# Moving the down-weight splits, re-ordering the drain and ending on a pair tile in an attention + mixture-of-experts kernel

## The reference

```python
x = x + xattn(ctx, layernorm(x), side)         # x: 4 x 1024 x 256, ctx: 4 x 77 x 256, 16 heads
xf = layernorm(x).reshape(4096, 256)
probs = softmax(xf @ Wr)                        # 9 experts
topk_w, topk_idx = top_k(probs, 2)              # then normalised to sum 1
gate = silu(xf @ Wg[e]); hidden = gate * (xf @ Wu[e])     # 256 -> 704
out = sum over the 2 experts e of topk_w * (hidden @ Wd[e])
x = x + out
```

## Time and profile before

| | |
|---|---|
| median of 3 runs | 832.52 us (832.21 to 832.76) |
| profiled execution | 832.81 us, its span 831.2 us |
| granted clock of PE | 0.996 of full over the span |
| PE busy | 795.7 us, 96% |
| DVE, ACT, POOL busy | 667.6, 625.8 and 380.2 us |

### The profile page before, as it was taken

The page is one execution under the profiler, slowest core; times in us unless marked ns, Lnnn a source line. Parts: engine busy times, 40 slices in busy tenths (PEclk is TensorE's granted clock), DMA queues, the critical chain, the costliest instruction groups (busy, mean ns, idle before and its releaser), DMA issues.

```text
span 831.2 us, 19592 instructions
## 1 busy us (share of the span) xinstructions
PE 795.7 (96%) x6037; PEld 754.9 (91%) x6037; DVE 667.6 (80%) x1620; ACT 625.8 (75%) x1966; POOL 380.2 (46%) x534
## 2 busy tenths in 40 slices
PE   7999999999999999879999999999999999999993
PEld 6866999999999999779999999999999999999993
DVE  6778888888888887887878788787888877888771
ACT  4578898889889888655777778777778777777771
POOL 3021377688778767763334233442343424424232
PEclk9999999999999999999999999999999999999998
DMA  8065900401310020656575182255752654556211
GB/s 288 20 152 147 268 32 30 150 27 40 122 52 33 33 85 27 210 155 171 148 199 120 25 262 46 47 170 152 225 153 46 194 159 119 133 142 160 40 23 23
DMA packets 78044, 96.14 MB, mean 116 GB/s; under 512 B 10680, under 2 KB 65140, under 8 KB 77940
## 3 DMA queue, kind: packets, MB, share of 16 engines
q1 hardware_dynamic: 64179, 75.94, 29.7%
q0 software_dynamic: 13760, 18.96, 12.4%
HBM read 108.14 MB, written 31.29 MB: 168 GB/s over the span
## 4 chain that ended last, share of the span: by engine, by line
PE 82%; DVE 4%; issue 3%; SPq 3%; POOL 2%; DMA 2%; ACT 2%; DVEq 1%; POOLq 0%
PE banks L344 23%; PE banks L345 22%; PE banks L346 22%; PE banks L1357 4%; PE banks L1337 2%; PE banks L1514 2%; PE banks L1371 2%; PE banks L1311 1%; DMA expert_in<-blank 1%; POOL expert_in L878 1%; PE banks L1287 1%; ACT prob L1046 1%; DVEq L1544 1%; PE banks L1323 1%; SPq L657 1%
## 5 line engine op out<-in xcount | busy, mean ns | idle before, releaser
L344 PE MATMUL banks<-tok_t_hi,wgt_hi 128*128 128x256 f32 x704 | 199.7, 284 | 4.8 <-DVE hid_f L1988 1.9
L346 PE MATMUL banks<-tok_t_hi,wgt_lo 128*128 128x256 f32 x704 | 198.0, 281 | 0.0
L345 PE MATMUL banks<-tok_t_lo,wgt_hi 128*128 128x256 f32 x704 | 197.9, 281 | 0.0
L941 POOL DMA_INDIRECT result<-res,tok_id x72 | 117.7, 1635 | 161.2 <-ACT res L1179 129.9
L1046 ACT ACTIVATE prob<-banks,row_min 128x77 f32<-128x77 f32 x512 | 161.8, 375 | 2.9 <-DVE row_min L1711 2.9
L1980 DVE TENSOR_TENSOR wgt_lo<-wgt,wgt_hi 128x704 fp32r<-128x704 f32 x174 | 150.4, 905 | 14.7 <-ACT wgt_hi L1122 14.7
L344 PEld LDWEIGHTS banks<-tok_t_hi,wgt_hi 128*128 128x128 f32 x704 | 134.3, 191 | 7.9 <-issue 5.9
L346 PEld LDWEIGHTS banks<-tok_t_hi,wgt_lo 128*128 128x128 f32 x704 | 133.5, 190 | 0.0
L345 PEld LDWEIGHTS banks<-tok_t_lo,wgt_hi 128*128 128x128 f32 x704 | 133.4, 189 | 0.0
L1122 ACT ACTIVATE wgt_hi<-wgt 128x704 fp32r (+1 forms) x174 | 130.6, 801 | 0.5
L1046 ACT ACTIVATION_READ_ACCUMULATOR prob<-banks,row_min 128x1 f32 x512 | 131.0, 257 | 0.0
(11 more groups left out here) (274 smaller groups left out, 2131.3 us busy)
## 6 DMA issues: line engine op xcount, KB each, us to landing
wgt<-in_L_ffn_Wg SPq DMA_DIRECT2D x29, 704.0 KB
wgt<-in_L_ffn_Wu SPq DMA_DIRECT2D x29, 640.0 KB
wgt<-in_L_ffn_Wd SPq DMA_DIRECT2D x29, 640.0 KB
tok<-expert_in SPq DMA_DIRECT2D x32, 258.0 KB, 3.4
spare_wgt<-in_L_ffn_Wg SPq DMA_DIRECT2D x9, 704.0 KB, 4.2
spare_wgt<-in_L_ffn_Wu SPq DMA_DIRECT2D x9, 640.0 KB, 5.9
spare_wgt<-in_L_ffn_Wd SPq DMA_DIRECT2D x9, 640.0 KB, 4.3
valmat_f<-valmat_dram SPq DMA_DIRECT2D x4, 1197.0 KB, 6.3
```

What stands on the lines that cost most here:

```text
L344: nc.tensor.matmul(to, a[0], b[0], start=first, stop=False)
L345: nc.tensor.matmul(to, a[0], b[1], start=False, stop=False)
L346: return nc.tensor.matmul(to, a[1], b[0], start=False, stop=last)
L941: nc.gpsimd.indirect_dma_start(out, bass.IndirectOffsetOnAxis(ap=tok_id[:, t % NOTES, a:a + 1], axis=0), res[i][:, a, :], None, compute_op ...
```

## The change

1. **Down splits.** Pieces 4 and 5 of tile t are split in tile t's own step, behind `tok_move`/`tok_rest` in unit 1 of a pair, or behind the hidden split of a single; before, this stood in unit 2 of step t - 1, ahead of the last hidden split of t - 1. They have their own semaphores (`down_hi`, `down_split_made`).
2. **Drain.** DVE's end of phase 1 is written out by hand (`drain`): the early gate-and-up splits and `tok_rest(0)` are elsewhere, `allot` of the last block stands behind `hidden(0, 1)`, `table_ends` is apart from `table_counts`, and the other table parts stand later between tile 0's and tile 1's work. PE takes `ranks(T - 3)` behind `gate_up(0, 0)` and `down(0)` behind `gate_up(1, 2)`. The exponential of the gates of the last two blocks goes from ACT to POOL, as a power of e, and ACT loads the silu table once, behind the probabilities' rounding.
3. **Tails.** SP stores all nine; eight of them are now 128 rows.
4. **SP's order.** The first single's weights are loaded in the step of tile 4, not ahead of tile 3's refills; gate-and-up refills go before down refills.
5. **End.** The last tile is a pair. Its two result blocks lie in two banks, its `down` starts ahead of the last hidden unit, and each block is scaled and added as soon as it is done.

The core of the diff goes through SP, POOL, ACT, PE (`down` of the last tile) and DVE:

```diff
-SINGLES_AFTER = (2, 6, 10, 13, 17, 21, 24, 28)
+SINGLES_AFTER = (2, 5, 9, 12, 16, 19, 23, 26)
...
-            for e in range(POOL_TAILS, E):
-                store_tail(sp, e, tails_stored)
+            for e in range(E):
+
+                blocks = WB if e == E - 1 else 1
+                row = sp.value_load(tail_row[0:1, e:e + 1], min_val=0, max_val=E * REGION - W)
+                sp.dma_start(expert_in[bass.ds(row, blocks * P), :].rearrange("(a p) d -> p a d", p=P), blank[:, 0:blocks, :]
+                             ).then_inc(tails_stored, 16)
...
+                refill_gate_up(t)
+                if t == EARLY + 1:
...
+                    load_single_gate_up(0)
+                    load_single_down(0)
                 if t > EARLY:
                     refill_down(t - 1)
-                refill_gate_up(t)
...
+            def gap_power(t, c):
...
+                nc.gpsimd.tensor_tensor(scaled[:], scaled[:], y_rstd[:], ALU.mult).then_inc(gap_scaled, 1)
...
+                nc.gpsimd.tensor_tensor(power[:], euler[:], scaled[:], ALU.pow).then_inc(gap_exp_done, 1)
...
+            def round_down(t, src):
+
+                act.wait_ge(*weights_loaded(t, False))
+                if t > EARLY:
+                    act.wait_ge(down_done, t - 1)
+                for p0, p1 in PIECES[2 * KT:]:
+                    nc.scalar.activation(wgt_hi[half_of(t)][:, p0:p1], src[:, p0:p1], ACT.Copy).then_inc(down_hi, 1)
...
                 for u in range(UNITS):
                     silu(t, u)
-                    if ahead:
+                    if ahead and u < UNITS - 1:
                         round_pieces(t + 1, u, src)
                     hid_round(t, u)
-                    if u == UNITS - 2 and t:
-                        tok_move(t + 1)
+                    if u == UNITS - 2:
+                        if t < NT - 1:
+                            tok_move(t + 1)
+                        if t >= EARLY:
+                            round_down(t, own)
...
+                if t == NT - 1:
+                    inner(0, 0, FC - 2)
+                    pe.wait_ge(res_ready, BLOCKS_TO[t])
+                    inner(1, 0, FC - 2)
+                    pe.wait_ge(hid_ready, UNITS_TO[t + 1])
+                    for a in range(blocks):
+                        inner(a, FC - 2, FC - 1)
+                        last_inner(a).then_inc(down_done, 1)
+                    return
...
+            for s in range(T + 1):
+                step(s, s)
+            drain()
+            table_ends()
+            hid_rest(0, 0)
             table_counts()
...
             hidden(0, 2)
             hid_rest(0, 1)
-            table_rows()
+            table_tiles()
             hidden(1, 0)
-            hid_rest(0, 2)
             early_down_rest()
+            hid_rest(0, 2)
+            tok_rest(2)
+            settle()
+            hidden(1, 1)
+            table_experts()
+            table_rows()
```

More of the change, by code:

```diff
@@ L15 @@
+import math
 from contextlib import ExitStack
@@ L557, in late_vals, with result_bank @@
             return range(SOON_VALS + s * LATE_VALS, min(SOON_VALS + (s + 1) * LATE_VALS, VALS))
[L559 to L564, removed]
+        def result_bank(t, a):
+            if t == NT - 1 and a:
+                return bank[7 - t % 2][:, 0:D]
+            return bank[6 + t % 2][:, a * D:(a + 1) * D]
         block = ctx.enter_context(nc.Block())
@@ L1084, in step @@
                     softmax_exp(s, c, 2)
-                if has(s, 3):
+                if s == T:
+                    tok_move(0)
+                    early_round(0)
+                if has(s, 3) and s - 3 < T - POOL_GAPS:
                     act.wait_ge(gap_ready, s - 2)
@@ L1208, in single_step @@
                 if not last:
-                    round_pieces(t + 1, 2, src)
-            for s in range(T + 4):
+                    round_down(t, spare_wgt[:])
+            for s in range(T + 2):
                 step(s, s)
+            silu(0, 0)
+            early_down_round()
+            hid_round(0, 0)
             silu(0, 1)
-            hid_round(0, 0)
+            tok_move(1)
             hid_round(0, 1)
@@ L1217, in _ @@
             hid_round(0, 2)
-            for t in range(1, NT):
+            silu(1, 0)
+            hid_round(1, 0)
+            silu(1, 1)
+            tok_move(2)
+            silu(1, 2)
+            hid_round(1, 1)
+            hid_round(1, 2)
+            res_move(0)
+            for t in range(2, NT):
                 if t == EARLY:
@@ L1458, in step @@
                     val(m)
-                if has(s, 3) and s < T + 2:
+                if has(s, 3) and s != T and s < T + 2:
                     ranks(s - 3)
@@ L1531, in single_step @@
                 hid_turn(t)
-            for t in range(1, NT):
+            for u in range(UNITS - 1):
+                gate_up(1, u)
+            tok_turn(2)
+            gate_up(1, UNITS - 1)
+            down(0)
+            for t in range(2, NT):
                 if is_pair(t):
@@ L1776, in step @@
                     find_most()
-                if s == T + 1:
-                    early_rest(1)
-                elif s == T + 2:
-                    hidden(0, 0)
                 if has(s, 2):
@@ L1804, in step @@
                     prob_rest(s - 2, c - 2, NG - 1)
+                if s == T:
+                    tok_rest(0)
+                    early_rest(0)
                 if has(s, -1):
@@ L2071, in _ @@
             table_slots()
-            hidden(1, 1)
+            hidden(1, 2)
             hid_rest(1, 1)
-            tok_rest(2)
             single_segments()
-            hidden(1, 2)
             hid_rest(1, 2)
```

212 lines of the change are left out of this document (134 added, 78 removed).

## The result

| | before | after |
|---|---|---|
| median | 832.52 us (832.21 to 832.76, 4 runs by now) | 822.07 us (820.95 to 823.93, 4 runs) |
| profiled execution, its span | 832.81, 831.2 us | 822.03, 820.3 us |
| ratio of times | | 0.9876, 95% interval 0.9864 to 0.9888 |

The account below looks back on a forecast made before the run. The kernel was taken as PE-bound, with some 14 us of gaps in three places. Terms 5.9 + 2.6 + 0.3 + 2.8 = 11.6 us off 832.8 give 821.2, said as 821.0 us; range 817.5 to 825.5.

Parts of the forecast that it names:

- singles: At seven singles, PE's gap ahead of `down` shrinks from 1.19 to 0.35: 0.84 each, 5.9 us in all.
- drain: Start of tile 3: DVE splits its tokens 3.2 us earlier, at 390.8; less 0.6 for unseen waits, 2.6 us gained.
- tile 5's tokens: PE's wait of 0.31 at 412.48 goes, as the first single's loads stand behind these tokens: 0.3 us.
- end: PE's last waits fall from 3.3 to 0.7, and 0.2 comes behind its last matmul: 2.8 us.
- The three 0.22 waits that I left standing: PE's waits two tiles behind a single, taken to stay; were they to go, some 0.4 us each.
- the sign named was 0.7: After the change, PE's waits from 420 to 800 should be about 0.7 us in all.
- Costing the move at nothing: The moved down pieces, 1.8 us on DVE in unit 1, fit its 1.96 us of idle time: no cost.
- the sign named for it: DVE should be idle for under 0.5 us ahead of `hid_f` in unit 2 of a pair.
- The 0.6 that I kept back for the power of e: 0.6 us taken off the drain's 3.2 for unseen waits, with the power of e in POOL's queue.
- the turn and 52 matmuls of 0.12 take it to 390.3 to 391.8: After waiting 2 to 3 us for tile 3's tokens, PE ends its own path then, next to DVE's 390.8.
- term 1's mechanism: At a single, moved down pieces let DVE's last hidden split end about 1.3 us sooner, ahead of PE: 0.84 each.
- The 0.2 for the stretch behind PE's last matmul: At the end, block 0's result comes 0.6 us ahead of the last, so 0.2 us was taken for this stretch.

Follow-up runs that it names:

- experiment 2: Changed kernel with the down splits of tile t + 1 back in unit 2 of step t, ahead of the last hidden split: 829.25 us, ratio 0.9942.
- experiment 3: Changed kernel with the singles in their old places, a single last, and the plain down and order at the end: 823.39 us, ratio 0.9877.
- Experiment 7: Changed kernel with a single's down pieces split ahead of its own hidden split, not behind it: 820.55 us, ratio 0.9840.
- experiment 1: The changed kernel run again with no edit: 822.93 us, ratio 0.9873 to the kernel before.
- 4: Changed kernel with tile 3's tokens ahead of pair 0's weights in SP's queue: 826.06 us, ratio 0.9908.
- 9: Changed kernel with tile 3's tokens loaded by POOL's queue and pair 0's down weights behind their landing: 822.74 us, ratio 0.9864.
- 10: Changed kernel with tokens loaded by POOL, the singles' last table behind tile 3's token split, and a single's down pieces ahead of its hidden split: 819.50 us, ratio 0.9829.
- 6: Changed kernel with pair 0's down weights issued only when tile 3's tokens have landed: 822.81 us, ratio 0.9863.
- 8: Changed kernel with the singles' last table behind tile 3's token split and pair 0's down weights behind the tokens' landing: 822.61 us, ratio 0.9872.
- 12: Changed kernel with block 29's normalising and routing back ahead of tile 0's token and weight splits in step 32: 821.35 us, a single run.
- 5: Changed kernel with 22 more matmuls of 128x256 filling PE's pause ahead of tile 3's token turn: 821.99 us, ratio 0.9856.
- 11: Changed kernel with 22 more matmuls in PE's pause at tile 3 and a single's down pieces ahead of its hidden split: 819.06 us, ratio 0.9822.

## Why the prediction came out as it did

| term | forecast | measured, by token turns of the two profiles |
|---|---|---|
| singles | 5.9 | 6.1 for seven (0.87 each) |
| drain | 2.6 | 1.9 at tile 4's turn (399.63, now 397.72) |
| tile 5's tokens | 0.3 | 0.45 (12.85 us from turn to turn, then 12.40) |
| end | 2.8 | 2.4, what is left of 10.9 us |

Only the singles and the end were undone by runs of their own (experiments 2 and 3). The drain's and tile 5's shares are read from token turns; no run takes them back.

- **Singles.** The mechanism holds, by the trace and by its own undoing (experiment 2). The three 0.22 waits that I left standing became four of 0.37 (1.5 us in all, where the sign named was 0.7), and these had a cause that I had not looked for: DVE runs from a single's down split to the tokens two tiles on without a pause. Experiment 7 moved that split and they went.
- **Unit 1.** Costing the move at nothing was right: away from the singles PE's list of waits is empty from 415 to 805. But the sign named for it did not come. DVE is idle ahead of `hid_f` in unit 2 for 1.1 us on average in 19 tiles (20.3 us in all), not under 0.5, so the moved splits took less of DVE's slack than the working has it.
- **Drain, DVE's side.** 390.8 forecast, 390.75 measured; tables and the held splits came as laid out. The tails were issued at 1.12 us apiece, not 1.25, and ended at 373.6, not 375.6; nothing hung on it, as the table came at 375.0. The 0.6 that I kept back for the power of e was not used there.
- **Drain, PE's side.** This is the step that was mis-sized: "the turn and 52 matmuls of 0.12 take it to 390.3 to 391.8". The pause was forecast (2 to 3 us; 2.77), but not that PE might come out of it at 1.2 GHz. That is 1.4 us in the profiled execution: tile 3 starts 1.3 us after DVE's 390.75, and the drain is 1.9. In the execution without the fall (experiment 1) PE is still the last to end, by 0.3 us (391.28 against 390.98), and tile 4's turn came at 396.94, which is a drain of 2.7. The 0.6 kept back for something else covered about half of the fall; that the term came so near is in part luck.
- **End.** The size was nearly right, its parts were not. 0.99 of the 3.3 us of waits belonged to term 1's mechanism: it was the eighth single's gap. What the new end itself gives is about 1.1 us in the span, and not to be told apart in the timing (experiment 3). The 0.2 for the stretch behind PE's last matmul is 0.1 by the spans (11.02 and 10.90).
- **Tile 3's tokens** stay the open end of the drain. Issue order (4), issuing engine (9, 10) and the load behind them (6) either leave them landing at 383.4 to 385.2 or make the weights late: 1.7 MB of weights and tokens wait for the pairs' table at 375. Getting the table earlier was not tried.

## What to carry to other kernels

When PE comes out of a pause, count what it does next at both of its clocks, and ask which chain then ends last. A pause that can't be removed can be filled with matmuls into a bank that is written afresh anyway; here the mean clock was then 0.995 or 0.996 in all nine runs. Before giving a wait at the end of a kernel to the edit made there, read what releases it: the same releaser elsewhere means the same mechanism. And an idle stretch on the engine that later ends last (1.33 us on DVE here) is a place to move work to, even if PE waits for something else just then.

## What the runs showed of the hardware

- **The granted clock falls behind some pauses of the same length and not behind others.** The profiled executions, by PE's pause at tile 3 and the time from its turn to tile 4's:

| pause, us | turn to turn, us | experiment |
|---|---|---|
| 2.77, 2.6, 3.5, 3.6, 3.2, 3.0, 3.0 | 13.78, 13.90, 13.68, 13.87, 13.86, 13.59, 13.71 | first profile, 3, 2, 6, 7, 8, 9 |
| 3.2, 2.6 | 12.38, 12.62 | 1, 12 |
| 2.2 | 13.04, clock 1.00, held by DVE | 10 |
| 0.7, 0.7 | 12.38, 12.38 | 5, 11 |
| 6.3, ahead of tile 3's first matmul | 7.44 from there to tile 4's turn, for 5.66 | 4 |

  So a pause of 2.6 to 3.6 us is a risk of 1.2 to 1.5 us, not a certainty; with 0.7 it was not seen. The clock fell 2.3 to 4.9 us after PE had gone idle, in experiments 6 and 7 only when PE was at work again (by 1.4 and 1.1 us). All nine runs of the two filled kernels have a mean clock of 0.995 or 0.996, where the changed kernel's eight have 0.991 to 0.996. The fall at tile 3 does not make all of that spread. In each profile the clock is also at 0.50 for the last 6 to 9 us of the span, behind PE's last matmul, where it costs nothing; this takes 0.004 to 0.006 off the mean, and the fall at tile 3 another 0.002, which gives the 0.994 of the first profile. Runs at 0.991 must have been low for longer, and where is not shown: none of them was profiled, and the kernel before has mean clocks from 0.991 to 0.996 too.
- **At a granted clock of 1.00 matmuls of 128x256 are 0.118 to 0.120 us apart in most tiles, and 0.113 behind each of the eight singles in the changed kernel** (440.76 to 443.03 for 20 of them). Behind four singles some 55 of the next pair's matmuls run at this pace, and then PE waits 0.37. Behind the other four some 50 do so one tile later, right behind the hold of 0.2, and in experiment 7 these are back at 0.120. What sets the pace is open.
- **POOL's division holds some of DVE's instructions beside it:** `xn` (1.55 for 0.48) and the weight pieces (1.95 for 1.28), but not `tok_rest(0)` (0.68), in one slot of one run each (experiment 12).
